# Gathered message sums in a graph layer: a circle of 8 pairs of tiles in place of 35, gathers without a wait for earlier ones, and no tile fetched by TensorE

## The reference

```python
h = jnp.maximum(_layernorm(x, axis=-1), 0.0)
hW = jnp.einsum('nd,tdf->tnf', h, W_edge) + b_edge[:, None, :]
msg = hW[etypes, src]
seg = dst * T + etypes
counts = jax.ops.segment_sum(jnp.ones(msg.shape[0]), seg, num_segments=N * T)
msg = msg / counts[seg][:, None]
agg = jax.ops.segment_sum(msg, dst, num_segments=N)
hN = jnp.einsum('nd,tdf->tnf', h, W_node) + b_node[:, None, :]
out = x + jax.nn.relu(hN[ntypes, jnp.arange(N)] + agg)
```

## Time and profile before

| what | value |
|---|---|
| median of 3 runs | 623.2 us (619.66 to 623.7) |
| the profiled execution's own time | 623.44 us |
| its span | 621.5 us |
| busy: TensorE, DVE, POOL, ACT | 434.3, 363.0, 405.8, 172.7 us |
| indirect gathers on POOL | 368 |
| TensorE's granted clock, mean | 0.857 of full speed |

### The profile page before, as it was taken

The page is one execution under the profiler, slowest core; times in us unless marked ns, Lnnn a source line. Parts: engine busy times, 40 slices in busy tenths (PEclk is TensorE's granted clock), DMA queues, the critical chain, the costliest instruction groups (busy, mean ns, idle before and its releaser), DMA issues.

```text
span 621.5 us, 9756 instructions
## 1 busy us (share of the span) xinstructions
PE 434.3 (70%) x3143; PEld 351.9 (57%) x3143; DVE 363.0 (58%) x913; ACT 172.7 (28%) x402; POOL 405.8 (65%) x384
## 2 busy tenths in 40 slices
PE   0269849977786675776776776767766776776687
PEld 0169628865565563665564565555645564565477
DVE  5966778876635545645645545646545646545633
ACT  2922424423313303213203213213203203303300
POOL 8067775666765576766766765766766766776760
PEclk9755559997977977978987978988898978988979
DMA  5541154333323313223323223223223323323320
GB/s 149 147 108 51 38 165 163 120 117 111 111 64 112 114 51 104 74 91 119 91 80 109 78 89 114 81 90 111 87 83 112 90 81 112 104 64 116 112 55 13
DMA packets 32497, 60.35 MB, mean 97 GB/s; under 512 B 7416, under 2 KB 22836, under 8 KB 29236
## 3 DMA queue, kind: packets, MB, share of 16 engines
q1 hardware_dynamic: 19372, 34.83, 17.1%
q0 software_dynamic: 11776, 24.14, 14.2%
q10 hardware_dynamic: 1296, 0.71, 0.5%
HBM read 56.01 MB, written 3.65 MB: 96 GB/s over the span
## 4 chain that ended last, share of the span: by engine, by line
DMA 57%; issue 17%; PE 16%; POOL 6%; DVE 2%; ACT 1%; SPq 1%; POOLq 0%; DVEq 0%; ACTq 0%
DMA G<-h_table,src_t 56%; POOL G L390 6%; PE out_ps L337 6%; PE acc L693 5%; PE misc L276 2%; PE out_ps L328 1%; DMA xs<-in_x_dram 1%; ACT union_a L543 1%; SPq L402 1%; PE misc L337 1%; PE node_ps L317 0%; POOLq L505 0%; PE out_ps L330 0%; DVE bsel L907 0%; PE misc L328 0%
## 5 line engine op out<-in xcount | busy, mean ns | idle before, releaser
L390 POOL DMA_INDIRECT G<-h_table,src_t x368 | 392.2, 1066 | 198.3 <-DMA G<-h_table,src_t 113.6
L693 PE MATMUL acc<-oh,G 128*128 128x384 f16 (+1 forms) x784 | 148.7, 322 | 150.6 <-issue 83.5
L973 DVE TENSOR_TENSOR S<-S,acc 128x384 f32 x196 | 108.2, 552 | 207.5 <-PE acc L693 207.0
L693 PEld LDWEIGHTS acc<-oh,G 128*128 128x128 f16 x784 | 75.3, 105 | 214.1 <-issue 124.2
L337 PE MATMUL out_ps<-w_all,union_a 128*128 128x128 f32 x768 | 120.7, 324 | 0.0
L337 PEld LDWEIGHTS out_ps<-w_all,union_a 128*128 128x128 f32 x768 | 116.7, 240 | 0.8
L964 DVE TENSOR_SCALAR oh<-iota,seg 128x224 f16<-128x224 f16 (+1 forms) x396 | 102.7, 313 | 10.3 <-issue 10.3
L283 ACT ACTIVATE G<-misc 128x256 f16<-128x256 f32 x24 | 9.2, 384 | 317.4 <-PE misc L276 306.7
L276 PE MATMUL misc<-hh,union_c 128*128 128x256 f16 x600 | 79.5, 278 | 0.0
L276 PEld LDWEIGHTS misc<-hh,union_c 128*128 128x128 f16 x600 | 59.7, 100 | 6.2
L296 ACT ACTIVATE dg<-id,wmask 128x128 f16<-128x128 f16 x200 | 60.7, 386 | 0.0
(11 more groups left out here) (97 smaller groups left out, 171.1 us busy)
## 6 DMA issues: line engine op xcount, KB each, us to landing
union_b<-rc_table SPq DMA_DIRECT2D x25, 1024.0 KB, 4.8
G<-h_table,src_t POOLq DMA_INDIRECT x368, 2.6
h_table<-hh SPq DMA_DIRECT2D x5, 320.0 KB, 2.6
src_row<-in_src_dram SPq DMA_DIRECT2D x24, 64.0 KB, 2.9
out_dram<-os SPq DMA_DIRECT2D x24, 64.0 KB
xs<-in_x_dram SPq DMA_DIRECT2D x4, 320.0 KB, 5.1
w_all<-in_L_gnn_W_node_dram SPq DMA_DIRECT2D x1, 512.0 KB
xs<-in_x_dram SPq DMA_DIRECT2D x1, 256.0 KB
```

Source lines behind the costliest of these rows:

```text
L390: nc.gpsimd.indirect_dma_start(out=G[:, slot, :], out_offset=None, in_=h_table[:, :], in_offset=bass.IndirectOffsetOnAxis(ap=index, axis=0 ...
L693: last = nc.tensor.matmul(window[:, :, 0:w], G[:, 2 * g_slot + a, part * D:(part + 1) * D], oh[:, o, a, 0:R * w].rearrange("p (t n) -> p t ...
L973: nc.vector.tensor_tensor(span, span, acc[bank][:, 0:R * W].rearrange("p (t n) -> p t n", n=W), ALU.add).then_inc(s_add, 1)
```

## The change

`G` is used as a circle of 8 pairs (SLOTS); it stays as large as it was, and the circle lies at its end. From pair 8 on POOL waits for the sums of the pair eight before, and for nothing else: no gather waits for an earlier one to land. The wait for `mask_ready` moves to the branch that this input does not take. There are 16 `landed` semaphores in place of 8. All 392 tiles, the padding one included, are gathered by POOL; the row loads, comparisons, matmuls and copies of the fetched tiles, their tiles and the table of node numbers go.

```diff
-    NEAR = 3
-    TURN = 8
+    SLOTS = 8
+    TURN = 2 * SLOTS
...
-        def sp_load_row(sp, b, p):
...
-        def dve_fetch(dve, b, p, use, part):
...
-        def pe_fetch(pe, b, part):
...
-        def act_fetch(act, b):
...
         def slot_of(pair):
-            return (pair + BODY) % (BODY + LATE)
-
-        def is_fetched(pair, a):
-            return a == 1 and pair != PAIRS - 1 and pair >= LATE and (pair - LATE) % PPB == PPB - 1
+            return BODY + LATE - SLOTS + pair % SLOTS
...
@@ gpsimd
             for j in range(LATE):
                 for a in range(2):
-                    gather(pool, 2 * (BODY + j) + a, src_t[:, 2 * j + a:2 * j + a + 1],
+                    gather(pool, 2 * slot_of(j) + a, src_t[:, 2 * j + a:2 * j + a + 1],
                            landed[2 * j + a])
             pool.wait_ge(flag_ready, 1)
             bad = pool.value_load(flag[0:1, 0:1], min_val=0, max_val=FLAG_MAX)
-            pool.wait_ge(mask_ready, 1)
             with pool.If(bad < 1):
-                for n in range(2 * LATE - NEAR):
-                    wait_landed(pool, n)
                 for pair in range(LATE, PAIRS):
-                    if pair >= LATE + BODY:
-
-                        pool.wait_ge(pair_mm, pair - LATE + 1)
+                    if pair >= SLOTS:
+
+                        pool.wait_ge(pair_mm, BODY + pair - SLOTS + 1)
+                        pool.sem_inc(issuing, 1)
                     for a in range(2):
-                        if not is_fetched(pair, a):
-                            n = gathers_upto(pair, a)
-                            wait_landed(pool, n - NEAR)
-                            pool.sem_inc(issuing, 1)
-                            gather(pool, 2 * slot_of(pair) + a, src_t[:, 2 * pair + a:2 * pair + a + 1], landed[n % TURN])
+                        n = 2 * pair + a
+                        gather(pool, 2 * slot_of(pair) + a, src_t[:, n:n + 1], landed[n % TURN])
             with pool.Else():
+                pool.wait_ge(mask_ready, 1)
...
@@ scalar
-                nc.scalar.activation(node_of, node_col[:, :].unsqueeze(2).to_broadcast([P, NB, P]),
-                                     ACT.Copy).then_inc(count_set, 1)
...
-                        act_fetch(act, b)
...
@@ tensor
                     for a in range(2):
-                        if not is_fetched(pair, a):
-                            wait_landed(pe, gathers_upto(pair, a))
+                        wait_landed(pe, 2 * pair + a)
...
-                        if u % PPB == PPB - 1:
-                            pe.wait_ge(fetched, 4 * i + u // PPB + 2)
-
...
-                        if v in (4, 5, 6):
-                            pe_fetch(pe, 4 * i + g, v - 4)
...
@@ vector
-                dve.wait_ge(count_set, 2)
...
-                        if v in (1, 2, 3):
-                            dve_fetch(dve, 4 * i + g, g % 2, 2 * i + g // 2, v - 1)
```

More of the change, by code:

```diff
@@ L139, in gnn_layer @@
             "p (n c) -> p n c", n=WQ)
[L141 to L147, removed]
         dg = sb("dg", [P, 2, K, P], F16)
@@ L223, in gnn_layer @@
         os_free = sem("os_free")
-        row_in = [sem("row_in0"), sem("row_in1")]
-        row_used = sem("row_used")
         count_set = sem("count_set")
-        fetch_oh = sem("fetch_oh")
-        fetch_mm = sem("fetch_mm")
-        fetched = sem("fetched")
         stored = [sem("stored0"), sem("stored1")]
@@ L249, in sp_load_rc @@
                          ).then_inc(rc_in[p], 16)
-        def sp_load_row(sp, b, p):
[L253 to L257, removed]
-        def dve_fetch(dve, b, p, use, part):
[L260 to L269, removed]
-        def pe_fetch(pe, b, part):
[L272 to L279, removed]
-        def act_fetch(act, b):
-            act.wait_ge(fetch_mm, b + 2)
-            nc.scalar.activation(G[:, 2 * slot_of(LATE + PPB * b + PPB - 1) + 1, :], misc[:, 0:2 * D],
-                                 ACT.Copy).then_inc(fetched, 1)
         def sp_store(sp, b, p, use, rows=P):
@@ L375, in slot_of @@
         def slot_of(pair):
-            return (pair + BODY) % (BODY + LATE)
-        def is_fetched(pair, a):
-            return a == 1 and pair != PAIRS - 1 and pair >= LATE and (pair - LATE) % PPB == PPB - 1
-        def gathers_upto(pair, a):
-            return 2 * pair + a - sum(is_fetched(p, 1) for p in range(pair))
+            return BODY + LATE - SLOTS + pair % SLOTS
         def wait_landed(engine, n):
@@ L417, in _ @@
             with sp.If(bad < 1):
-                sp_load_row(sp, 0, 0)
-                sp_load_row(sp, 1, 1)
                 sp.wait_ge(cnt_ready, 1)
@@ L432, in body @@
                     for g in range(4):
-                        if not (first and g < 2):
-                            sp_load_row(sp, 4 * i + g, g % 2)
                         sp_load_rc(sp, 4 * i + g, g % 2)
@@ L479, in _ @@
             pool.wait_ge(consts, 6)
-            nc.gpsimd.iota(node_col[:, :], pattern=[[P, NB]], base=-MID, channel_multiplier=1,
-                           allow_small_or_imprecise_dtypes=True)
             nc.gpsimd.memset(S[:, :, :], 0.0).then_inc(zeroed_s, 1)
@@ L570, in _ @@
             nc.scalar.activation(nt_t[:, :], misc[:, 0:NB], ACT.Copy).then_inc(et_out, 1)
-            for s in (zeroed, hn_ready, fetched):
+            for s in (zeroed, hn_ready):
                 act.sem_inc(s, 1)
@@ L654, in _ @@
                 pe.sem_inc(s, 2)
-            pe.sem_inc(fetch_mm, 1)
             pe.sem_inc(pair_mm, BODY)
@@ L910, in _ @@
             dve.sem_inc(mask_ready, 1)
-            for s in (scaled, fin, os_free, row_used):
+            for s in (scaled, fin, os_free):
                 dve.sem_inc(s, 2)
```

## The result

The changed kernel takes **594.5 us** (median of 4 runs, 594.06 to 596.66) against 623.1 for the kernel before (619.66 to 623.7): ratio 0.956, 95% interval 0.953 to 0.960. Forecast were 590 us and a range of 578 to 612. The profiled execution (596.66 us, span 594.9) is the slowest of the four; the other spans are 592.3 to 592.8.

A forecast was written before the change was run, and what follows sets the result against it. Bound: the pace at which POOL's gathers deliver tiles. 70.4 + 467.6 + 28 + 4.4 + 1 = 571.4 us for the last gather; with the tail 587.9, plus 1.9 outside the span: 590 us, range 578 to 612.

The forecast's parts named there:

- The head start: POOL, its circle full after 16 gathers, waits for pair 0; loses some 18 us, gather 16 starts at 70.4.
- The remaining gathers: On POOL, from gather 16 to gather 391: 375 steps x 1.247 us = 467.6 us.
- Landing and slot waits to nothing: On POOL, waits on gathers landing (65 us) and the slot wait (3.6 us) go; delay sits in the circle's slack.
- Stretch by the scale: Gathers on POOL held by DVE's scale (L353): 1.2 us a block x 24 = 28 us; bounds 0 and 2.2.
- The stuck gather: The single long gather of 5.36 us at 73.16 on POOL stays: 4.4 us of stretch.
- What follows is untouched: After the last sums, the tail to the end of the span stays as before: 16.4 us.
- rival C: TensorE, idler without the fetch, gets a lower clock: 599 us with a third of idle kept, 657 with all; chance 0.07.
- The fetch at nothing: The removed fetch's matmuls, DVE work, ACT copies and row loads lie beside POOL's pace: nothing; its 8.6 us stretch goes.
- The rule of the lock: A skill's rule by which DVE's scale waits for a running gather: about 2.0 us a block, not 1.2; 609 us.
- A: POOL can't hand over a further gather until an older lands; the stall returns inside the gather: 651 us, chance 0.09.
- B: Stretch of gathers by DVE grows to 2.0 us a block in another phase: 609 us, chance 0.12.
- rival D: Pace stays, set by the reciprocals' burst and PE's idle time, not POOL: 638 us, or about 622; chance 0.06.

The follow-up runs named there:

- the scale from PSUM: Changed kernel with 23 of the 25 scales reading their second factor from PSUM: 665.1 us, against 683.9 for the changed kernel in the same series.
- the circle of 35: Changed kernel with a circle of 35 pairs in place of 8, run twice: 715.1 and 714.7 us, the second 1.073 times the kernel before.

## Why the prediction was right, point by point

- *The head start* (POOL idle about 18 us, gather 16 at 70.4): 18.06 us beyond the 0.30, at 71.20. Right; gather 16 is 0.8 late.
- *The remaining gathers* (375 steps x 1.247 = 467.6): 575.76 - 71.20 less the stretches is 468.3, 1.249 each. Right. The forecast puts down 0.944 + 0.30 for its step, which is 1.244 and would give 466.5; the 1.247 it used is nearer.
- *Landing and slot waits to nothing*: right, none over 0.1 us after gather 16.
- *Stretch by the scale* (28): 30.9 on 23 gathers, 1.34 each in place of 1.2. The term that was mis-sized most: in the block shown the scale came 0.90 ahead of the next gather, not 1.0.
- *The stuck gather* (4.4) 3.9; *L964's* (1), with all other stretch, 1.5.
- Together the last gather starts at 575.76 in place of 571.4. To that come 1.0 of landing and hand-over at the last full pair, and 1.6 in the tail: 7.0 us on the span, of which 2.1 to 2.6 are this execution's own against the three others. On the median the forecast is 4.5 us low. *"What follows is untouched"* is the step that failed in the tail: the instructions are the same, but TensorE, now idle 1.7 to 2.0 us between pairs, had 0.66 of its clock for the node matmuls in place of 1.00, and they took 3.45 us in place of 1.96. That is rival C in small; here nothing of POOL's hides it.
- *The fetch at nothing*: the sum that leaves it out comes out, so POOL's pace hid it both ways as far as the sum can tell, and the fetch's own stretch of 8.6 went.
- *The rule of the lock* (609 us): what the row said held. The scale is 2.29 us long wherever it falls, so DVE does not wait for a running gather, and the gather's delay of 1.34 is nearer to 1.2 than to 2.0. Of the Trainium skill's rule (SBUF — State Buffer, "Who interferes with whom") the scale from PSUM bears out another part: two inputs in SBUF are what contends with GpSimd's reads. With both there 23 gathers were stretched by 40.7 us, with one in PSUM none.
- *Rivals A, B and D* are out where the kernel before takes 623 us: gathers stay at 0.944 with POOL never waiting for a landing (up to 6.8 us after issue, so by 6.8 / 1.25 five or six under way), the scale stretches one gather in 23 blocks, by 1.34 on average and not 2.0, and the block's pace fell to 21.46.
- One of the signs named did not show: TensorE's waits all on the gather's DMA. The profile's waits put 15.6 us of its idle time before the sums to that DMA and 143.0 to "issue", that is to nothing that it can name.

There is luck in the 590 as well: the series it was measured in had the kernel before at 623 us, as its profile did. What the prediction did not have is that all of it holds only where the other engines' instructions keep coming beside a stream of gathers. Where the kernel before took 662 to 712 us the changed kernel was not faster (1.025, interval 1.006 to 1.044). That is rival D by another mechanism: POOL's waits go, and the others can't follow. Each part was then worth something else: the fetch's removal cost 26 us where 21 were reckoned, the small circle gained some 31 in place of costing 18, and the landing wait cost 8 in place of 65 (against a run on another chip).

Open: what makes that condition. The profile names no releaser, it was there in all five series on four chips, and the page shows the loads of instructions unchanged (28 packets, 0.46 MB and 0.3% of the DMA engines' time in the kernel before at 623 us and at 706.8). Open too are the parts' single prices where the kernel before takes 623 us: that POOL's path set the time before and after, and what each part is worth on it, rests there on the accounting of the two profiles alone. By that accounting the fetch kept with a circle of 8 would take 573 us; it wasn't tried there.

## What to carry to other kernels

When one queue's instructions are the bound, add its timeline up before anything else: count times base duration, plus idle time beyond the base gap by releaser, plus stretch. It closed to within a microsecond here, and each part of a change is then a term that can be forecast. Taking away a wait for an earlier transfer to land gives back its idle time only if there are slots that can take up the delay instead. As an estimate from this case, the slots needed are the longest delay over the pace (6.8 us over 1.25, some six tiles), not all that fit; fewer than 16 were not tried. And work that runs ahead is not free: before filling a deep circle at start, look whether the other engines stand idle between instructions that have no wait between them. Last, take the kernel before along in every series of runs: here it showed that a gain of 4.4% was gone when nothing in the two kernels had changed.

## What the runs showed of the hardware that was not expected

- Matmuls of one batch without any wait between them came one per 2.80 us beside running gathers, and 392 of them took 31.02 us (0.08 each) without gathers, in the same condition. On DVE and ACT waits with a remote releaser of up to 69 us stand in the same stretch of the circle of 35.
- The same program can be in or out of this condition over whole series of runs: 619.66 to 623.7 us in one, 662 to 712 in five others, while a gather (0.94 us), an add (0.55) and the scale (2.29) keep their durations. A gain of 4.4% measured in the one was not there in the other.
- A DVE instruction of 2.29 us with both operands in SBUF holds up a gather that starts inside it: the gather ends 0.81 us after the instruction. With one operand in PSUM it doesn't, at the same length. A gather that started 0.35 us ahead of the instruction kept its 0.94.
